# Attention scores in four small array tiles: plain keys and queries as the stationary operand instead of masked copies

## The reference, cut to what matters

```python
x = x + attn(layernorm(x))          # causal linear attention: phi(rope(q)), phi(rope(k)); num/den by prefix sums
x = x + xattn(layernorm(x), ctx, ctx, mask)   # softmax(q k^T / sqrt(8)) v per head, q = layernorm(x), k = v = ctx
x = x + moe(layernorm(x))           # shared SwiGLU plus the top 2 of 8 experts, hidden 256
```

## Time and profile before

| | |
|---|---|
| median of 3 runs | 1055.57 us (1054.49 to 1060.03) |
| the profiled execution | 1064.24 us, its span 1062.0 us |
| granted TensorE clock, mean | 0.926 |
| busy, share of the span | PE 81%, PEld 66%, DVE 69%, ACT 55%, POOL 56% |
| the pipeline's first scores, by step | 28.7, 51.3, 76.6, 110.6, 148.4, ... 568.6 us; about 38.2 us a step from 148.4 on |

### The profile page before, as it was taken

One profiled execution on the slowest core, in us unless ns is written; L12 is line 12 of the kernel. 1 busy time (PEld: TensorE's weight loads), 2 busy tenths in 40 slices (PEclk: granted clock), 3 DMA queues, 4 the chain that ended last, 5 costly groups with the idle time before them and its releaser, 6 DMA issues.

```text
span 1062.0 us, 27434 instructions
## 1 busy us (share of the span) xinstructions
PE 863.1 (81%) x9293; PEld 695.8 (66%) x9294; DVE 730.3 (69%) x1980; ACT 583.0 (55%) x1116; POOL 598.8 (56%) x792
## 2 busy tenths in 40 slices
PE   4779989898888988898888875987988898888810
PEld 3567777677677776677766654876866676666610
DVE  2346768878887888787798986667555555555545
ACT  3567658667666667666766553532355555545410
POOL 4455435865766666676585665247066666665620
PEclk9789889999998999999999987898999999999965
DMA  9011011111101101102101103111122222222169
GB/s 250 2 41 41 2 41 44 32 49 46 55 24 51 52 22 51 51 22 60 46 29 52 59 14 120 34 37 33 31 72 76 69 70 72 68 68 65 52 182 298
DMA packets 92389, 65.96 MB, mean 62 GB/s; under 512 B 8943, under 2 KB 84472, under 8 KB 92288
## 3 DMA queue, kind: packets, MB, share of 16 engines
q1 hardware_dynamic: 75424, 43.46, 15.2%
q0 software_dynamic: 8416, 16.93, 4.8%
q10 hardware_dynamic: 8448, 4.20, 1.3%
HBM read 42.44 MB, written 22.56 MB: 61 GB/s over the span
## 4 chain that ended last, share of the span: by engine, by line
PE 41%; DVE 25%; issue 12%; ACT 10%; POOL 5%; DMA 3%; another core or an unknown queue 3%; SPq 1%; POOLq 0%; ACTq 0%; DVEq 0%
PE bank L802 6%; PE pair_x L784 4%; DVE mx L1318 3%; PE bank L700 3%; DMA Kblk<-mixed 3%; PE pair_x L688 2%; DVE b_xn L1302 2%; PE bank L460 2%; PE pair_y L688 2%; PE bank L792 2%; PE pair_x L519 2%; PE bank L538 2%; PE bank L630 2%; DVE Ex L1322 2%
## 5 line engine op out<-in xcount | busy, mean ns | idle before, releaser
L1216 POOL DMA_INDIRECT mixed<-f_y,f_x x135 | 133.7, 990 | 54.3 <-issue 31.8
L1135 POOL DMA_INDIRECT routed<-c_row,c_idx x128 | 127.5, 996 | 40.8 <-issue 40.8
L802 PE MATMUL bank<-Qblk,Am 128*128 x540 | 93.5, 296 | 30.1 <-DVE Am L1573 30.0
L802 PEld LDWEIGHTS bank<-Qblk,Am 128*128 128x128 f32 x540 | 71.0, 191 | 71.3 <-issue 71.1
L1067 POOL TENSOR_TENSOR tick<-minus_half 128x1 f32<-128x1 f32 x151 | 30.4, 201 | 138.2 <-DVE c_place L1403 72.4
L1092 POOL TENSOR_TENSOR Qblk<-qT,con 128x512 f32<-128x512 f32 x64 | 67.1, 1054 | 71.5 <-DVE qT L1270 71.2
L930 ACT COPY ExT<-pair_x 128x1024 f32<-128x1024 f32 x64 | 64.3, 1005 | 56.9 <-PE pair_x L613 44.2
L613 PE MATMUL pair_x<-con,Ex 128*128 128x128 f32 x512 | 72.4, 287 | 19.4 <-ACT Am L898 16.4
L1318 DVE TENSOR_REDUCE mx<-pair_y 128x16 f32<-128x1024 f32 x64 | 78.2, 1221 | 12.7 <-PE pair_y L599 11.7
L898 ACT ACTIVATE Am<-pair_x 128x1024 f32<-128x1024 f32 x64 | 64.8, 1013 | 40.1 <-remote 21.4
L613 PEld LDWEIGHTS pair_x<-con,Ex 128*128 128x128 f32 x512 | 57.7, 146 | 43.7 <-issue 42.3
(11 more groups left out here) (214 smaller groups left out, 2283.5 us busy)
## 6 DMA issues: line engine op xcount, KB each, us to landing
f_x<-routed SPq DMA_DIRECT2D x135, 65.0 KB
ctxD<-in_ctx SPq DMA_DIRECT2D x32, 256.0 KB, 4.2
ctxP<-in_ctx SPq DMA_DIRECT2D x16, 256.0 KB, 2.8
maskB<-in_mask_BxS_if SPq DMA_DIRECT2D x16, 256.0 KB, 4.1
Cblk<-mixed SPq DMA_DIRECT2D x16, 256.0 KB, 5.2
Kblk<-mixed SPq DMA_DIRECT2D x16, 256.0 KB, 6.1
block_out<-X ACTq DMA_DIRECT2D x16, 256.0 KB, 5.8
mixed<-f_y,f_x POOLq DMA_INDIRECT x135
```

The costliest lines, as they stand in the source:

```text
L802: ins = pe.matmul(banks[F_O][:, 0:D], f_hT[:, u % 3, c * P:(c + 1) * P], wdn[:, bass.ds(e, 1), c, :].rearrange("p o d -> p (o d)"), start= ...
L1135: pool.indirect_dma_start(routed[:, :], bass.IndirectOffsetOnAxis(ap=c_idx[:, par, t, n:n + 1], axis=0), c_row[:, par, t, n, :], None, bou ...
L1216: pool.indirect_dma_start(mixed[:, :], bass.IndirectOffsetOnAxis(ap=f_x[:, u, D + 1:D + 2].bitcast(I32), axis=0), f_y[:, u, :], None, boun ...
```

## The change

The masked copies are gone. The plain keys are written by DVE (`a_feature`) straight into `Kt`, and ACT's `b_norm_evac` copies the plain queries once into `Qt`; `a_k_spread` falls away. Each score matmul is split in two by quarter: it takes only the 32 rows of one quarter and 64 stationary columns, and writes 64 output partitions of its bank. The four tiles of the array are rows 0-31 with columns 0-63, rows 32-63 with columns 64-127, rows 64-95 with columns 0-63, rows 96-127 with columns 64-127. The mask matmuls in front stay as they are (64 rows, 128 columns).

```diff
-        KQ = sb("KQ", [P, 2, 2, GS, C, T])
-        Kc, Qc = KQ[:, 0], KQ[:, 1]
+        KQ = sb("KQ", [P, E * 2 * INTER])
+        Kt, Qt = (KQ[:, n * 2 * GN:(n + 1) * 2 * GN].rearrange("p (m n) -> p m n", m=2) for n in range(2))
...
                 if j == 0:
-                    pe.wait_ge(S["a_kcd"], C * a + C)
+                    pe.wait_ge(S["a_ph"], 2 * a + 2)
...
                     for i in range(2):
-                        half = slice(i * T, (i + 1) * T)
-                        ins = pe.matmul(banks[i][:, s * RH * T:(s + 1) * RH * T],
-                                        Kc[half, par, 2 * j + s, :, :].rearrange("p c n -> p (c n)"),
-                                        Qblk[half, j, s, :, :], start=False, stop=(s == 1))
+                        for c in range(C):
+                            rows = slice((C * i + c) * DH * RH, (C * i + c + 1) * DH * RH)
+                            ins = pe.matmul(banks[i][c * T:(c + 1) * T, s * RH * T:(s + 1) * RH * T],
+                                            Kt[rows, par, (2 * j + s) * T:(2 * j + s + 1) * T],
+                                            Qblk[rows, j, s, :, :], start=False, stop=(s == 1))
...
-                        half = slice(i * T, (i + 1) * T)
-                        ins = pe.matmul(banks[2 + i][:, s * RH * T:(s + 1) * RH * T],
-                                        Qc[half, par, k, :, :].rearrange("p c n -> p (c n)"), Kblk[half, j, s, :, :],
-                                        start=False, stop=(s == 1))
+                        for c in range(C):
+                            rows = slice((C * i + c) * DH * RH, (C * i + c + 1) * DH * RH)
+                            ins = pe.matmul(banks[2 + i][c * T:(c + 1) * T, s * RH * T:(s + 1) * RH * T],
+                                            Qt[rows, par, k * T:(k + 1) * T], Kblk[rows, j, s, :, :],
+                                            start=False, stop=(s == 1))
...
-            def a_k_spread(f, par):
-                act.wait_ge(S["a_ph"], 2 * f + 2)
-                if since(f, 2):
-                    act.wait_ge(S["a_s"], NP * (f - 1))
-                for c in range(C):
-                    act.activation(Kc[:, par, :, c, :], rot[:, 0:GN].rearrange("p (b n) -> p b n", n=T), ACT.Copy,
-                                   scale=quarters[:, c:c + 1]).then_inc(S["a_kcd"], 1)
...
-                for c in range(C):
-                    act.activation(Qc[:, par, :, c, :], by_sequence(FRONT1), ACT.Copy, scale=quarters[:, c:c + 1])\
-                        .then_inc(S["b_qcd"], 1)
+                act.copy(Qt[:, par, :], banks[FRONT1][:, :]).then_inc(S["b_qcd"], 1)
...
-                if since(f, 1):
-                    dve.wait_ge(S["a_kcd"], C * f)
...
                 if since(f, 2):
                     dve.wait_ge(S["a_qb"], NP * (f - 1))
-                for m, (bank, dst) in enumerate(((FRONT1, qT[:, par, :]), (FRONT0, rot[:, 0:GN]))):
+                    dve.wait_ge(S["a_s"], NP * (f - 1))
+                for m, (bank, dst) in enumerate(((FRONT1, qT[:, par, :]), (FRONT0, Kt[:, par, :]))):
```

More of the change, by code:

```diff
@@ L73 @@
 SB_ALIGN = 32
-CONST = {"ident": P, "late": T, "cos": HALF, "turn": C * HALF, "row": RH, "quarter": C, "half": C, "order": E, "before": P,
+CONST = {"ident": P, "late": T, "cos": HALF, "turn": C * HALF, "row": RH, "half": C, "order": E, "before": P,
          "region": E, "place": GT * TOP, "upto": E * E, "tile": TILE_MAX}
@@ L95, in shape_constants @@
     part("row")[:] = (p // DH % RH)[:, None] == np.arange(RH)[None, :]
-    part("quarter")[:] = (p // (DH * RH) % C)[:, None] == np.arange(C)[None, :]
     part("half")[:] = (p // T)[:, None] == np.arange(C)[None, :]
@@ L166, in const @@
             return con[:, CONST_AT[name]:CONST_AT[name] + CONST[name]]
-        ident, late, cos, turn, row, quarters, halves, order = (
-            const(n) for n in ("ident", "late", "cos", "turn", "row", "quarter", "half", "order"))
+        ident, late, cos, turn, row, halves, order = (
+            const(n) for n in ("ident", "late", "cos", "turn", "row", "half", "order"))
         a_stat = sb("a_stat", [P, GT, 6])
@@ L242, in decoder_block @@
         t_row = sb("t_row", [1, TILE_MAX], I32)
-        wup = KQ[:, :, :, :, :, :].rearrange("p a m b c n -> p (a m b c n)").rearrange("p (e m i) -> p e m i", e=E, m=2)
+        wup = KQ[:, :].rearrange("p (e m i) -> p e m i", e=E, m=2)
         wdn = Qblk[:].rearrange("p m s r n -> p (m s r n)").rearrange("p (e c d) -> p e c d", e=E, c=CH)
@@ L268, in decoder_block @@
             a_st a_ag a_ve a_pw a_rsd a_xnd a_xnT_ps a_xnTd a_qk_ps a_qkd a_v_ps a_vd a_r2 a_r1 a_mn a_ex a_ph
-            a_qT_ps a_kT_ps a_kcd a_qb a_s a_am a_av a_dn a_rc a_yd a_yT_ps a_yTd a_o a_x1
+            a_qT_ps a_kT_ps a_qb a_s a_am a_av a_dn a_rc a_yd a_yT_ps a_yTd a_o a_x1
             b_st b_ag b_ve b_pw b_rsd b_xnd b_qT_ps b_qcd b_in b_cT_ps b_cTd b_bi b_kb b_cb b_s b_mx b_sb
@@ L566, in b_ctx_T @@
                 if not isinstance(h, int) or h >= 1:
-                    pe.wait_ge(S["b_qcd"], C * h)
+                    pe.wait_ge(S["b_qcd"], h)
                 else:
@@ L584, in b_scores @@
                 if j == 0:
-                    pe.wait_ge(S["b_qcd"], C * b + C)
+                    pe.wait_ge(S["b_qcd"], b + 1)
                     pe.wait_ge(S["b_bi"], b + 1)
@@ L830, in _ @@
             act.copy(gate_sum[:, :], banks[1][:, E:2 * E]).then_inc(S["set_cp"], 1)
-            def by_sequence(bank):
-                return banks[bank][:, :].rearrange("p (b n) -> p b n", n=T)
             def normalise(i, src, rs, nm, dst, s_rs, s_xn):
@@ L998, in step @@
                         a_exp(f)
-                    if k == 7 and on(f):
-                        a_k_spread(f, odd)
                     if k == 7 and on(h):
```

## The result

The changed kernel takes 1064.46 us (median of 20 runs, 1057.45 to 1070.5), the kernel before 1056.12 us beside it (20 runs, 1051.51 to 1060.56). The ratio is 1.0064 with a 95% interval of 1.0045 to 1.0084: slower by 0.64%, or 6.8 us, where +1.6 us was forecast. The ratio compares the runs as a whole (their means differ by 6.8 us); the two medians lie 8.3 us apart, so 6.8 is good to some 2 us either way. The time lies inside the range and 7.5 us above the predicted 1057. The profiled execution of the changed kernel took 1064.75 us; the one of before, 1064.24 us, lies above all 20 of its kernel's runs. So the two traces, laid side by side, can hardly show the difference of the medians. They show how the work changed; what it costs has to come from timed runs.

What follows compares the result with a forecast made beforehand. No engine is full, so waits decide, with DVE last at the step's end. Relief -1.6, fill +1.4, full steps +1.3 and tail +0.5 gave +1.6 us on the 1055.57 median: 1057, range 1046 to 1074.

Steps and rivals of the forecast that it cites:

- Four tiles at once: PE's score calls: four tiles run side by side, still 0.86 us a call; two-at-a-time rival +80 us, 1136, chance 0.10.
- The switch: PE, between mask and score shapes: 0.12 us each (0.09 to 0.15), 143 switches, 17 us of PE time.
- Where it lands: PE's waits cover eight of nine switches per full step: +1.3 us over eleven steps, fill +1.4, tail +0.5.
- The cover: Full step: PE's waits for ACT's masks, `c_row` and `c_xfT` hide eight of nine switches while they last.
- my sum: Whole kernel: -1.6 + 1.4 + 1.3 + 0.5 = +1.6 us, giving 1057.
- the signs that I had named for being wrong: A call taking 1.7 us, growing pauses in `a_project_v`, or a step period moving by over 0.5 us.
- ACT's relief: ACT loses 31 us of work, 2.0 us a step; worth nothing in a full step because DVE is last.
- The rival in which it reaches the path: If ACT sets the step's end: -8 us, 1048, or 1037 if DVE's L1368 shrinks too; chance 0.16.
- The fill: First two steps, without the query copy on the path: first scores 0.9 us earlier, next step 0.7, together -1.6 us.
- the switches land on the path, in part: PE's switches uncovered by waits: all of them +15.5 us, 1071, half 1064; chance 0.24 in part or whole.

Runs made afterwards that it cites:

- One shape: Changed kernel with both attentions' mask matmuls in the scores' 32 by 64 tiles; 1005.87 us, ratio 0.9975 on one chip, 1060.5 us, 1.0013 on another.
- switch alone, large scores: Kernel before with mask matmuls in 32 by 64 tiles and scores left at 64 by 128; 1079.41 us, ratio 1.0223.
- PE's side alone: Kernel before with scores in four tiles of 32 by 64, ACT still making the masked copies; 1017.04 us, ratio 1.0095.

## Why the prediction came out as it did

**Four tiles at once: right.** This was the part with most at stake. The rule of the Trainium skill (TensorEngine Tiling (Array Packing), section Restrictions and Gotchas), that different row tiles can't access the same PSUM bank simultaneously, would have made 1136 us. Four records share 0.45 us in the trace, the two quarters of a half writing different partitions of one bank, so in that form the rule did not hold here; the trace decides.

**The switch: right in kind, too small in size.** Predicted were 0.12 us (0.09 to 0.15) a switch and 17 us of PE in all. Over all calls of the full steps with no wait inside, the median from the mask's start to the start of the group of another shape behind the scores is 1.18 us before and 1.34 us after: 0.16 us, beyond the upper bound of 0.15. Where `b_scores` follows directly it is 1.09 and 1.35 us: another 0.10 for the second switch. At the clock's lower level (0.50 granted, the call at 110.61 before and at 110.37 after) it is 2.24 and 2.45 us, so 0.2 there. Of the 0.16 some 0.09 is the gap ahead of the first score record, which I had from the earlier trace rows; the rest is in the first scores themselves, whose first slot of four is longer (0.45 us for it, against 0.38 for the first pair of before). 128 x 0.16 + 15 x 0.10 = 22 us of PE instead of 17. One shape brings the call back to 1.20 us. The Trainium skill, page TensorEngine Tiling (Array Packing), section Tiling Modes, says that a change of the tiling mode drains the engine; the gap agrees with it, and the runs put 0.16 us on the whole.

**Where it lands: this is the step that failed.** I had only one switch of nine on the path of a full step, and +3.2 us in all (1.3 in the full steps, 1.4 in the fill, 0.5 at the end) of 17, about a fifth. What the timed runs show:

| | PE work added by switches (us) | time lost (us) | share | time lost at equal clock (us) |
|---|---|---|---|---|
| switch alone, large scores | 29.8 | 23.6 | 79% | 17 |
| PE's side alone | 22.0 | 9.6 | 44% | 7 |
| changed minus one shape, first chip | 19.4 | 8.2 | 42% | 7 |
| changed minus one shape, third chip | 19.4 | 6.6 | 34% | 6 |

The left column is calls times what a call grew by, from the traces: 22.0 as above, 19.4 what is left of it when one shape's 128 x 0.02 us is taken off, and 128 x 0.22 us plus what follows at `j` 3 for the first line. The next is the ratio (or the difference of two) times the time of before. The last is what is left by the line through the runs' mean clocks, to some 2 us (3 in the first line). So 34 to 44% lands, or about a third at equal clock, not a fifth; with 22 us that is 7 to 10 us, and 6.8 were measured with ACT's relief set against it.

The cover itself was counted rightly, as far as the clock is full: such a full step takes 37.8 to 38.1 us in the traces of the kernel before, of the changed one and of the switch alone, with 32.7, 34.0 and 34.3 us of PE's work in it. Not even the one uncovered switch of nine shows there. What failed is the sum over the rest. The fifth group's first scores stand at 148.4 and 145.7 us in two traces of the kernel before, and at 150.5, 153.6 and 148.0 in three of the changed one (147.7 and 148.1 with one shape): the fill ends some 4 us later, where my sum had it 0.2 us earlier (+1.4 for the switches, -1.6 of relief). The full steps take 420.2 and 418.8 us before, and 420.8 and 422.3 in the traces of the changed kernel beside them, some 2 us more for the 1.3 of my sum; in the trace from the first chip they take 428.9, with a clock of 0.92 for 0.96. Behind the full steps the spans do not differ (493 and 491 us, then 492 and 492). Each of these is one execution, and one kernel's traces lie 3 us apart. My sum was worked out with waits read in a step at full clock, and where the clock is lower PE has fewer of them: the step at 222.6 of the kernel before, at a clock of 0.91, has 3.7 us free and not 5.1. That this is why the work lands there is argued; the stages and the clocks are measured. The waits without a named cause stay open: 5.5 us stand before L614 in the changed kernel where 0.6 stood, and those in `a_project_v` are 12.6 and 11.2 us in two traces before and 10.4 and 13.4 in two after. Of the signs that I had named for being wrong none came clearly: no call takes 1.7 us at full clock, the pauses in `a_project_v` are as above, and the period is 38.3 us.

Nor is it settled which of the two attentions pays. Without the first one's switches the kernel was as slow as the changed one (1.0067, on another chip than either comparison with the full one shape), which may mean that the second's scores stand on the path, those that `b_shift` waits for. The mirror experiment was not run.

**ACT's relief: right.** Worth nothing in a full step was predicted; without any effect of the tiles it is 0.11% with an interval over zero. The rival in which it reaches the path has fallen: the 0.86 us before `c_exp` stood at 0.88, neither filled nor lengthened by the 0.7 us that I expected, and L1353 still ends last there.

**The fill: right in mechanism.** First scores 1.03 us earlier (0.9 predicted), and so in every trace (27.7 to 28.1 for 28.6 and 28.7). The second step's start, 51.27 and then 47.21, shows no more than how much traces scatter. None of the lead lasts: the fifth group's first scores come later than before, as above, so the -1.6 us of my sum were not there at the fill's end.

**The rival that came nearest** is "the switches land on the path, in part": half of them gave 1064 (by its own price, half of 15.5 us, 1063), and 1064.46 was measured. There is luck in how near that is: 34 to 44% landed and not half, and of more switch work than it had. Its ground, that PE has the largest share of the chain, held better for the whole kernel than my count of covers did; its test, the waits of a full step, would have spoken against it. With the whole of the switches, 1071 was about as wrong as 1057. That the time fell into my range is no merit of the sum either: the range was wide enough for this rival.

**A version that beats both** was not found. One shape comes out at 0.9975 (0.9963 to 0.9987) and 1.0013 (0.9984 to 1.0041) of the kernel before on two chips: it is faster than the changed kernel both times, and a gain over the kernel before was not repeated.

## What to carry to other kernels

Look at what shape stands ahead of and behind the matmuls that you retile: four small tiles cost the same as two large ones here, and the change between them and the mask's 64 by 128 cost 0.16 us a call, 128 times; giving the neighbours the same shape took that back. A list of waits from one step is cover for a step like it, at that clock: here it held for full steps at full clock and missed what the fill, and the stretches with a lower clock, had to pay. So count the cover in every stage and at both levels of the clock, and look at the mean clock of the timed runs before a time is put down to the edit alone. About 30 us of work taken from ACT, which waits for others at the step's end, changed nothing that could be told (-0.11%).

## What the runs showed of the hardware that was not expected

- A change of the tile's shape from the mask's 64 by 128 to 32 by 64 costs more than the gap that the records show: 0.16 us, some 0.09 of it ahead of the first record and the rest inside the first slot; 0.2 us at the clock's lower level.
- It costs more still from small to large: 0.22 us a call with masks of 32 by 64 and scores of 64 by 128 (1.40 us instead of 1.18).
- Two row tiles wrote one PSUM bank at the same time, on different partitions of it: four records in 0.45 us. The same partitions were not tried.
- The mean granted clock goes with the kernel as well as with the run: 0.910 over 6 runs with the switch alone, 0.930 over 23 of the kernel before on that chip, and 3 to 5 us of time go with each 0.01.
- Two chips of the same kind differ by 48 us (1008 and 1056 us) with the same kernel, 36 to 41 of them in the loop over the routed experts (214 us, and 250 to 255), and the pauses in `a_project_v` are in the traces of the slower ones only. The ratios agree all the same (1.0056 and 1.0064 for the changed kernel).
